# A two-layer graph network kernel: seven one-hot picks in every iteration of layer 1, in place of six and seven in turn

## What is computed

```python
h = relu(layernorm(x))
# layer 0: an edge network, a mean by destination, a node network
m = relu(concat(h[src], edge_attr_16) @ w1a + b1a) @ w1b + b1b
x = x + node_mlp(h, segment_sum(m, dst) / max(count, 1))
h = relu(layernorm(x))
# layer 1
m = relu(h[src] + edge_attr_32)
x = x + (1 + eps) * h + segment_sum(m, dst)
```

## Time and profile before

| what | us |
|---|---|
| median of 3 runs | 7706.84 |
| lowest and highest | 7704.2, 7731.67 |
| the profiled execution's own time | 7755.14 |
| its span, first to last instruction | 7753.3 |
| layer 1's loop on PE, about | 4068 to 7734 |

### The profile page before, as it was taken

How to read it: one execution, slowest core, us unless ns; L and a number is a source line. 1 busy time by engine, 2 the same in 40 slices (tenths; PEclk the granted TensorE clock), 3 DMA queues, 4 the chain that set the end, 5 groups by cost and what they waited for, 6 DMA issues and landing times. The chain is left out here.

```text
span 7753.3 us, 135939 instructions
## 1 busy us (share of the span) xinstructions
PE 6671.4 (86%) x35037; PEld 5083.7 (66%) x35038; DVE 3953.2 (51%) x8138; ACT 4197.1 (54%) x8680; POOL 4584.7 (59%) x4850
## 2 busy tenths in 40 slices
PE   7888888888888888888888888888888888888888
PEld 5666666666666666666676666666666666666666
DVE  5444444444444444444455555555555555555555
ACT  5555555555555555555545555555555555555554
POOL 5666666666666666665635655556566556566665
PEclk8999999999999999999879999999999999999998
DMA  3222222222222222222211111111111111111111
GB/s 99 49 49 49 48 49 49 48 49 48 49 49 49 48 49 48 49 49 48 49 34 40 40 40 39 40 40 39 41 40 40 39 41 40 39 40 41 40 41 39
DMA packets 421789, 352.22 MB, mean 45 GB/s; under 512 B 112227, under 2 KB 379360, under 8 KB 421490
## 3 DMA queue, kind: packets, MB, share of 16 engines
q0 software_dynamic: 154016, 161.08, 11.6%
q1 hardware_dynamic: 118558, 113.68, 5.4%
q10 hardware_dynamic: 149172, 76.95, 3.7%
HBM read 342.82 MB, written 8.46 MB: 45 GB/s over the span
## 5 line engine op out<-in xcount | busy, mean ns | idle before, releaser
L882 PE MATMUL bank<-part_high,owner_hot 125*128 125x512 f32 (+1 forms) x10059 | 4073.0, 411 | 407.8 <-issue 322.8
L882 PE MATMUL bank<-part_low,owner_hot 125*128 125x512 f32 (+1 forms) x10059 | 3871.8, 399 | 315.5 <-issue 313.7
L861 POOL DMA_INDIRECT gathered<-projected_rows,index x2500 | 2368.4, 947 | 1542.7 <-issue 763.4
L861 POOL DMA_INDIRECT gathered<-hidden_rows,index x2313 | 2194.7, 949 | 1474.0 <-issue 637.0
L882 PEld LDWEIGHTS bank<-part_high,owner_hot 125*128 125x128 f32 x10059 | 2032.7, 202 | 913.7 <-issue 450.9
L882 PEld LDWEIGHTS bank<-part_low,owner_hot 125*128 125x128 f32 x10059 | 2039.9, 203 | 723.0 <-issue 384.2
L978 ACT ACTIVATE owner_hot<-owner_in,minus_piece 125x256 fp32r<-125x256 f32 (+2 forms) x5250 | 2132.7, 487 | 296.4 <-remote 104.7
L1161 DVE TENSOR_TENSOR sums<-sums,bank 97x48 f32 (+1 forms) x1250 | 252.5, 202 | 2289.9 <-remote 1523.4
L1004 ACT ACTIVATE messages<-gathered 128x384 f32<-128x384 f32 (+1 forms) x1250 | 531.3, 425 | 1369.3 <-DVE gathered L1154 888.5
L983 ACT ACTIVATE owner_hot<-owner_hot 125x1792 fp32r<-125x1792 f32 (+1 forms) x750 | 1228.1, 1637 | 23.8
L1116 DVE SCALAR_TENSOR_TENSOR hidden<-window_f,places,bank 128x512 f32<-128x512 f32 x625 | 464.9, 744 | 1171.9 <-remote 878.0
(11 more groups left out here) (119 smaller groups left out, 1994.0 us busy)
## 6 DMA issues: line engine op xcount, KB each, us to landing
edge_r<-in_edge ACTq DMA_DIRECT2D x620, 80.0 KB
owner_in<-owner_rows SPq DMA_DIRECT2D x250, 192.0 KB
gathered<-projected_rows,index POOLq DMA_INDIRECT x2500
gathered<-hidden_rows,index POOLq DMA_INDIRECT x2313
owner_in<-owner_rows SPq DMA_DIRECT2D x250, 128.0 KB
edge_r<-in_edge ACTq DMA_DIRECT2D x620, 40.0 KB
owner_in<-owner_rows SPq DMA_DIRECT2D x250, 64.0 KB
projected_rows<-projected SPq DMA_DIRECT2D x25, 168.0 KB
```

The costliest lines, as they stand in the source:

```text
L861: pool.indirect_dma_start(gathered_rows(k, row)[:, t, :], None, table, bass.IndirectOffsetOnAxis(ap=index[k][:, t:t + 1], axis=0)).then_in ...
L882: last = nc.tensor.matmul(bank[pick_home[home]][:, 0:(b.stop - b.start) * D], pick_hot(pick, j, odd(turn)), part[0:NP, b, :].rearrange("p ...
```

## The change

Both parities of layer 1 use the whole table. `ODD_ONLY` goes. A round of two iterations now has 14 picks, so the list of PSUM banks gets 14 entries.

```diff
-ODD_ONLY = PICK_TABLE[2]
 
 LAYER_PICKS = ((tuple(pick for pick in PICK_TABLE if pick.tile == TILES - 1),) * 2,
-               (tuple(pick for pick in PICK_TABLE if pick is not ODD_ONLY), PICK_TABLE))
+               (PICK_TABLE, PICK_TABLE))
...
             else:
                 LOOK, SELECT = 2, 1
-                pick_home = [0, 1, 2, 5, 6, 7] * 2 + [5]
+                pick_home = [0, 1, 2, 5, 6, 7, 0, 1, 2, 5, 6, 7, 2, 5]
```

## The result

The changed kernel takes 7640.36 us (median of 4 runs, 7636.88 to 7653.18), the kernel before 7710.22 us beside it: ratio 0.9901, 95% interval 0.9888 to 0.9913. It is 1% faster. I had forecast 2.9% slower, so the sign was wrong; "faster" had 0.12 of my chances.

A forecast was written before the change was run, and what follows sets the result against it. TensorE was taken to bound layer 1 by picks, scatters and stalls. Terms 218 + 12 + 1.5 - 6 = 226 us, added to the median 7706.84 us, gave 7930 us; 8-in-10 range 7820 to 8010, the forecast's own 7875 to 7980.

The forecast's parts named there:

- The step that failed: Layer 1's even iterations: TensorE's 5.59 us idle, against 1.98 in odd ones, comes from its own instruction stream, not slack.
- 0 on the path: GpSimd in layer 1: 63 fewer gathers only become more waiting for TensorE; 0 to -12 us if stalls go, -6 taken.
- What bounds the kernel: Layer 1's loop: bound by TensorE, by picks, scatters, and stalls that come once a pass of the body.
- A pick at a clock of 0.89, 3.46 us: TensorE, even iterations: each added pick takes 3.08 us at full clock, 3.46 at 0.89; 63 picks add 218 us.
- Stalls, 12 us more: TensorE's loop body in layer 1: 24 us more if stalls grow with the code, nothing if once a pass; 12 taken.
- Start of layer 1: ScalarE makes owner_hot for 384 columns, not 256, in the first even iteration; TensorE waits for it: +1.5 us.
- vector engine: Layer 1: 115 us of added vector engine work is hidden, since that engine has idle time.
- GpSimd's waits: Layer 1: GpSimd already waits 826 us for TensorE, and the removed gathers turn into more such waiting.
- the lower bound: Pick banks in layer 1: TensorE's 15.1 us of bank waits may go, 0 to -15 us; 0 was taken.
- Rival 1: Even iterations: the idle is slack from something slower, the added pick fills it, time stays at 7707 us; chance 0.08.
- Rival 2: Layer 1: GpSimd sets the pace; if its pauses are its own, 63 fewer gathers give 100 us, 7607; chance 0.12.
- The page's rule: Layer 1's loop: weight-load share measures TensorE's fullness; a third of its time free, sum near nothing.

The follow-up runs named there:

- before_18_gathers: Kernel before, but in layer 1's even iterations tile 3 of slot 1 is neither gathered nor picked (18 gathers in every iteration); ratio 0.9883.
- after_again: The changed kernel rerun unchanged, in a later sitting: 6405.09 us against 6217.47 us for the kernel before, ratio 1.0302.
- before_18_again: Kernel before without gather and pick of tile 3, slot 1, in layer 1's even iterations, rerun where the kernel before took about 6220 us; ratio 0.9997.

## Why the prediction was wrong

**The step that failed** is "An idle that depends on the place in the code and that no semaphore ends I take for something of TensorE's own instruction stream, not for slack". From it came, for the 63 gathers removed, "0 on the path" with at most 12 us of stalls to be saved, and "It lies on the path: no other engine's wait covers it" for the 218 us of picks. In the sittings that belong to the recorded times, the two terms are the other way round. The 63 gathers are worth 89 us (before_18_gathers), and the 63 picks nothing that can be measured; the two together, the change, gained 70 to 88 us in three sittings. The idle was slack after all, for a pick.

- *What bounds the kernel.* Nearly all of the chain was TensorE and "issue", and I read the whole of it as TensorE's bound. That an engine fills the chain did not make it the bound: with 750 us fewer of the work of L882, the line with 64.2% of the chain, the kernel got 113 us faster. Layer 1 takes 3666 us for 2313 gathers before, 3568 for 2250 after, 1.59 us each in both traces.
- *A pick at a clock of 0.89, 3.46 us.* As a price at the full clock 3.08 us was right: 2.98 us were measured where TensorE has no idle. In the stalled kind the clock wasn't a constant to divide by. It rose with the work, from 0.93 to 0.97: TensorE's busy time went up by 67 us, not by 194 or 218. Idle fell by 165 us, and the loop got shorter.
- *Stalls, 12 us more.* They were about 146 us less ("issue" waits of TensorE, 456.7 to 310.9 us). The 12 us, and the 24 us that it is half of, rest on stalls that grow with the code; no run shows that.
- *Start of layer 1, vector engine, GpSimd's waits.* Nothing in the new trace speaks against taking the first two as small or hidden. GpSimd's waits for TensorE, which I had expected to grow, stayed where they were: 826 us before, 354.3 + 472.5 us after. The bank waits did go, as the lower bound had it.
- *The rivals.* Rival 1 has the mechanism: the pick went into idle that something slower imposed. It lacks the gain. Rival 2 has the gain (7607 forecast, 7640 measured; 1.4 us a gather, not 1.59) and its sign (all iterations near 28.4 us: 28.75 and 28.35), but its condition, that the pauses are GpSimd's own, isn't shown. A case that joins them was missing: the gathers set the pace, and a pick fills the idle that they leave on TensorE. The even iterations, with 19 gathers and the long idle, pointed at it. I had even used them as an argument for both rivals, which I gave 0.20 together.
- *The page's rule.* Weight loads were busy for 66% of layer 1's loop, and I set the rule of the Trainium skill ("Trainium Kernel Development and Optimization", "Performance Expectations") aside. In the free kind, with no idle at all, their share is 2033.92/2600 = 78%. Against that, the 66% left about a sixth of TensorE's time to be had, not a third. The rule pointed the right way for the stalled kind. This case can't say that it is the better measure: busy matmul time, 87% there and 100% in the free kind, says much the same.
- *Right for the other kind, by luck.* The 63 picks cost 188 us where the kernel before takes 6218 us, close to the 194 us at the full clock. That both the forecast and this run say 3% is in part an accident, 226 us of 7707 and 188 us of 6218. The trace that I read was of the stalled kind.

**What stays open.** What makes the two kinds. The kernels, their inputs and the place of their loops don't, nor does the chip alone (chip 14 gave both). What else the machine did then isn't on record. In the stalled kind, whether GpSimd's time or the indirect gathers themselves set the pace, and whether broken runs of gathers help, weren't tried: the kernels for it ran in free sittings only.

## What to carry to other kernels

Idle with no releaser is not proof that an engine is bound by itself. Compare iterations that differ in one thing: here the iteration with less TensorE work and one gather more was the longer one, and the simple reading of that, the gather costs and the pick doesn't, was the true one for the times at hand. Take away each of the two by itself before you explain either. Where two engines are balanced against each other, a price holds only for the state in which it was measured, so rerun the kernel before beside every comparison and look at its absolute time first.

## What the hardware did that I had not expected

- The same program took 7641 to 7726 us in two sittings of the experiments, 23 to 24% longer than the 6218 us of the other three. In the long ones TensorE starts single matmuls up to 2.8 us apart in the middle of an accumulation; in the free traces of after_again and before_18_again no start in a pick is over 0.34 us behind the last one (3400 to 6000 us).
- In the stalled trace of the kernel before 118 of some 120 unbroken runs of eight or more gathers have a stall ("issue" idle of TensorE over 0.8 us), and 12 of the 93 runs of exactly seven. Half of the stalls end more than 1.7 us after the last gather of the run, none over 2.9 us.
- After a stall matmuls of 512 columns start 0.43 us apart, at 1.2 GHz, against 0.23 us. Taking 750 us of work away from TensorE lowered its mean clock from 0.93 to 0.84, adding 63 picks raised it to 0.97.
- Where TensorE's loop lies in its program made no difference: 0.9996 and 1.0005 for the kernel before, each with an interval of 0.1% to either side.
